# Message passing of a graph network: the block's own product opens its PSUM sum, a product of a zero column closes it

## The reference, cut to what matters

```python
h = node_embedding
for _ in range(DEPTH):                       # DEPTH = 3
    msgs = jnp.take(h, src, axis=0)
    msgs = jax.nn.relu(msgs @ W_edge + b_edge)
    agg = jax.ops.segment_sum(msgs, dst, num_segments=N_NODES)
    h = jax.nn.relu(jnp.concatenate([agg, h], axis=-1) @ W_agg + b_agg)
```

## Time and profile before

| | us |
|---|---|
| median of 3 runs | 6392.83 |
| the profiled execution's own time | 6391.64 |
| its span in the profile | 6389.9 |
| message passing, from the first to the last product L793 | 854.9 to 3439.8 |
| TensorE busy over the span | 4607.5 (72%) |
| GpSimd busy over the span | 3504.7 (55%) |

### The profile page before, as it was taken

How to read it: one execution, slowest core, us unless ns; L and a number is a source line. 1 busy time by engine, 2 the same in 40 slices (tenths; PEclk the granted TensorE clock), 3 DMA queues, 4 the chain that set the end, 5 groups by cost and what they waited for, 6 DMA issues and landing times. The chain is left out here.

```text
span 6389.9 us, 107350 instructions
## 1 busy us (share of the span) xinstructions
PE 4607.5 (72%) x19910; PEld 2847.6 (45%) x19911; DVE 3779.0 (59%) x12447; ACT 1894.9 (30%) x4118; POOL 3504.7 (55%) x3741
## 2 busy tenths in 40 slices
PE   5666657777677777667666777667777776888887
PEld 3444435555455555444443333334444443333333
DVE  7666633333333333333335888768888886777777
ACT  0222213333333333111111000022222222666666
POOL 1555544444344443444443555566666664888887
PEclk8888868888788888777778999955555556999999
DMA  0433435555445444433334888733333332333333
GB/s 29 132 129 127 132 111 156 154 152 151 135 149 153 150 149 146 117 106 109 107 106 129 269 268 270 253 88 99 99 98 99 100 98 76 103 105 105 105 105 94
DMA packets 732203, 840.14 MB, mean 131 GB/s; under 512 B 150205, under 2 KB 575272, under 8 KB 732068
## 3 DMA queue, kind: packets, MB, share of 16 engines
q1 hardware_dynamic: 619172, 619.89, 30.2%
q0 software_dynamic: 112896, 218.94, 13.4%
HBM read 439.86 MB, written 398.61 MB: 131 GB/s over the span
## 5 line engine op out<-in xcount | busy, mean ns | idle before, releaser
L756 POOL DMA_INDIRECT mp_gathered<-msg_rows,other_idx x1176 | 1116.6, 949 | 1463.7 <-PE bank L775 997.4
L775 PE MATMUL bank<-mp_edge_hot,mp_gathered 128*128 128x256 bf16 x5292 | 948.9, 310 | 517.9 <-issue 477.8
L775 PEld LDWEIGHTS bank<-mp_edge_hot,mp_gathered 128*128 x5292 | 558.8, 106 | 827.2 <-issue 718.1
L834 ACT ACTIVATE mp_h_out<-bank,mp_b_agg 128x256 f32<-128x256 f32 x588 | 278.5, 474 | 1488.9 <-PE bank L793 834.5
L522 POOL DMA_INDIRECT by_window<-so_pay,so_pos_i x392 | 394.0, 1005 | 426.3 <-issue 285.0
L868 DVE TENSOR_SCALAR mp_edge_hot<-digits,mp_first_col,column 128x256 bf16<-128x256 bf16 x1764 | 506.0, 348 | 144.5 <-PE bank L793 79.7
L793 PE MATMUL bank<-mp_h_in,mp_w_agg_h 128*128 128x256 f32 x1176 | 478.7, 495 | 110.2 <-issue 103.6
L1196 POOL DMA_INDIRECT at_kv<-kv_rows,kv_idx x392 | 387.4, 988 | 258.1 <-DVE at_prod L1350 141.5
L891 DVE TENSOR_TENSOR mp_msg_out<-mp_rest,mp_msg_out 128x256 bf16<-128x256 f32 x392 | 166.4, 424 | 590.4 <-ACT mp_msg_out L847 321.0
L1198 POOL DMA_INDIRECT at_q<-q_rows,node_idx x392 | 414.0, 1056 | 122.9 <-issue 122.9
L1475 POOL DMA_INDIRECT ff_agg<-at_rows,last_idx x392 | 413.9, 1056 | 98.6 <-issue 88.7
(11 more groups left out here) (216 smaller groups left out, 9177.7 us busy)
## 6 DMA issues: line engine op xcount, KB each, us to landing
mp_h_in<-h_cols SPq DMA_DIRECT2D x588, 128.0 KB
h_cols<-mp_h_out SPq DMA_DIRECT2D x588, 128.0 KB
msg_rows<-mp_msg_out SPq DMA_DIRECT2D x392, 192.0 KB
kv_rows<-pn_proj SPq DMA_DIRECT2D x98, 512.0 KB
msg_rows<-so_msg_out SPq DMA_DIRECT2D x98, 384.0 KB
h_cols<-so_h_out SPq DMA_DIRECT2D x98, 256.0 KB
pn_h_in<-h_cols SPq DMA_DIRECT2D x98, 256.0 KB
x_rows<-pn_x_b SPq DMA_DIRECT2D x98, 256.0 KB
```

The source lines that it names most:

```text
L756: pool.indirect_dma_start(gathered[:, r * PARTS * D:(r + 1) * PARTS * D], None, core.msg_rows[layer % 2], bass.IndirectOffsetOnAxis(ap=cor ...
L775: product = nc.tensor.matmul(agg_bank[k], gathered[:, bass.ds(at + d * D, D)], hot, start=(first and d == 0), stop=True, skip_group_check= ...
```

## The change

In `sum_edges` the fp32 product of the block's own columns now comes first and opens the sum. The wait for its operand `h_ld` comes with it, behind the wait for `h_ok`. The one-hot products follow, none of them with `start=True`. What closes the sum is a new bf16 product of 128 zero columns with one zero column into the first column of the bank; it adds zero and carries the increment of `win_mm`.

```diff
                         first, final = edge_tiles(pe, n, r, waits=False)
                         reached(pe, h_ok, wins + n - 1)
+                        pe.wait_ge(h_ld[r], 16 * (turns_done + j + 1))
+                        nc.tensor.matmul(agg_bank[r % 2], w_agg_h[:, :], h_in[r][:, :], start=True, stop=True, skip_group_check=True)
                         pe.wait_ge(edge_hot_ok, wins + n + 1)
                         pe.wait_ge(tile_in, layer * NT + first + ALWAYS)
                         for c in range(ALWAYS):
-                            added = add_tile(r % 2, first + c, edge_hot[r % HOTS][:, c, :], first=c == 0)
+                            added = add_tile(r % 2, first + c, edge_hot[r % HOTS][:, c, :])
                         added.then_inc(tile_mm[layer], 1)
                         further(pe, n, first, final, more)
-                        pe.wait_ge(h_ld[r], 16 * (turns_done + j + 1))
-                        nc.tensor.matmul(agg_bank[r % 2], w_agg_h[:, :], h_in[r][:, :], start=False, stop=True,
+                        nc.tensor.matmul(agg_bank[r % 2][:, 0:1], zero_cols[:, 0:D], zero_cols[:, 0:1], start=False, stop=True,
                                          skip_group_check=True).then_inc(win_mm, 1)
```

## The result

The changed kernel takes 6405.79 us in the median of 16 runs, the kernel before 6391.48 us in the median of 16 runs: the ratio is 1.0025, with a 95% interval from 1.0018 to 1.0031. That is +16 us by the ratio. The direction of the prediction was right and the time lies in its range; its size of +53 us was more than three times too large.

The account below looks back on a forecast made before the run. TensorE's sequencer, by its instruction count plus a slow stretch per chunk, was taken to bound message passing. Terms 41 + 15 - 3 = +53 us on 6391.64 us gave 6445 us (+0.8%), 80% range 6388 to 6500 us.

Parts of the forecast that it names:

- The bound: Message passing, some 2585 us: paced by the instructions TensorE's sequencer must issue, plus a slow stretch for each chunk.
- the order pays: Rival: the array ends the turn, so the product moved into idle gaps saves up to 139 us; 6311 us, chance 0.09.
- The lone waits: Blocks two to four of each turn: a semaphore wait becomes its own instruction, 0.10 us each, three a turn, +41 us.
- The closing product: End of each of 588 blocks: an added weight load and product at 0.025 us a pair, +15 us.
- The hold on `h_ok`: L786 at the block's head: no longer holding the sequencer on this semaphore gains 0 us; its records last 32 to 36 ns.
- the load's due time: Block's head: operand due 1.75 us earlier, 7.0 us after its load's issue; 0 us unless a load takes longer.
- Layer starts: The product runs while the first tiles come in, three times up to 1 us: -3 us, layer ends included.
- The step that failed: Turns beside gathers: the stretch set by the chunk's gathers keeps its length, so added instructions cost their fast price once.
- slow stretch: Part of each chunk beside gathers where TensorE's register instructions need from 1212.5 to 1217.3 us, some 0.69 us each.
- by number of instructions: Rival: the slow stretch counts instructions, not microseconds; 0.60 us a turn, 83 us, 6475 us (6500 with upper prices), chance 0.10.
- in slack: Rival: the turn's length hangs on the chunk, so added instructions cost only single microseconds; 6390 to 6395 us, chance 0.11.
- its last sign of being wrong: Loop turns: those with gathers grow by another amount than those without, so the slow stretch is no constant.

## Why the prediction had the direction right and the size wrong

**The bound** was read rightly (the mean of GpSimd's 133 waits is 7.5 us and not 7.4, which changes nothing). The sequencer's list is the turn: without gathers the change costs 54.9 us in time and 53.2 us between branches, and the array, which got 588 products more and a better order, takes no part in it there. The rival "the order pays" is out as a forecast, 6311 us against 6405.79 us. It priced one of a turn's four products, and what it names is there on a small scale: beside gathers on the first chip the new order gave back 13.5 us in two layers, where the prediction had the array get nothing back. Whether it is the idle array that pays was not isolated.

**The lone waits** were counted rightly (414) and priced somewhat low. On the first chip 368 of them cost 38 us, 0.10 us each, the value taken. Without gathers on the second the whole change comes to 0.129 us for each, and the start-to-start step is 0.125 to 0.126 us. The 0.1 us read for L50 in the earlier trace rows is a difference of two rounded times; unrounded it is 0.126 us (2557.695 to 2557.821). The rows would have allowed the upper bound of 0.13 us.

**The closing product** was priced too high. Forecast +15 us; measured -4 us [-8, +1] and +1 us [-6, +9]. The 0.025 us per pair of load and product was what remained of a stretch after an estimated step, and with steps of 0.115 us nothing remains. That the sum of 56 us was met without gathers is luck: one price was some 11 us too low and the other 15 us too high. The Trainium skill, "TensorE: Matmul & The Clock Gate", section "Wait — 56ns, not 53.3ns?", gives some 62 ns for each matmul with hardware decode off; the estimate of 36 us worked out from it lies further from the measured -4 and +1 us still.

**The hold on `h_ok`, at nothing,** was right: 0.9991 and 1.0006 without it. So was the load's due time. SyncE issued the load of the last block at 3445.10 us, its product started at 3452.35 us, and the sequencer went on at its pace.

**Layer starts, -3 us:** not to be seen. From the last branch of a layer to the first of the next it is 83.0 and 76.5 us before and 82.9 and 79.1 us after.

**The step that failed** is the one at the end of the sum: "I let it keep its length, so that the added instructions cost their fast price once." Beside gathers the five turns of the earlier trace rows grew by 0.16 us each in the place of 0.40, and all 132 by 0.09 us in the mean. So the turn is not the fast turn plus a slow stretch of constant length: the rest of it became shorter as instructions came in. Neither alternative that was named fits: by number of instructions the turn would have grown by 0.60 us, and the added work is not in slack, since lone waits still cost 19 to 31 us beside gathers. The prediction had named this itself as its last sign of being wrong, that the turn with gathers grows by another amount than the one without.

It is tempting to say that an added instruction is cheap in the slow stretch, where some register instructions last as little as 2 to 9 ns and not 36 to 46 ns. The trace of the changed kernel doesn't bear that out as the cause. Of its 414 lone waits in the loops, counted record by record, 319 last 51 ns, with a median step of 0.126 us to the sequencer's next own instruction; 66 last under 40 ns, 28 over 250 ns and one lies between. Two more traces of the same kernel give 310 and 327 in the place of 319. So three quarters of the waits pay the full price, 40 us by themselves, and yet the loops grew by 14.3 us. What was given back lies elsewhere in the turn.

Shown in its place is the amount: 55 us without gathers, 16 to 20 us with them; 13.5 us given back by the new order beside gathers where there is no slow stretch; and in the old order 19 us beside slow stretches for waits that come to 46 us at 0.126 us each. By what way the turn becomes shorter is open.

A block beside gathers in the changed kernel, PE's timeline from 1211 us, shows that the stretch itself looks as in the earlier trace rows: single one-hot products with "issue" ahead of each.

```profile
1214.71 0.28 PE L775 MATMUL bank<-mp_edge_hot,mp_gathered 128*128 128x256 bf16 x1 [0.96 <-issue]
1215.28 0.28 PE L775 MATMUL bank<-mp_edge_hot,mp_gathered 128*128 128x256 bf16 x1 [0.29 <-issue]
1216.00 0.39 PE L775 MATMUL bank<-mp_edge_hot,mp_gathered 128*128 128x256 bf16 x1 [0.43 <-issue]
1218.10 0.37 PE L775 MATMUL bank<-mp_edge_hot,mp_gathered 128*128 128x256 bf16 x1 [1.71 <-issue]
```

**Open** stays what the slow stretch is, why one of four chips has none, and why a turn beside gathers gives back part of what is added to it. The new order without any lone wait, in all three layers, was not run; with lone waits in the last layer alone it is even with the kernel before on three chips. No edit tried here beat the kernel before clear of noise.

## What to carry to other kernels

- Where a turn is paced by a sequencer, count its instructions, the waits first: two semaphores at one product make an instruction of 0.126 us at the sequencer's even pace, while a further small product behind others was free here. Put two waits on two neighbouring instructions that exist anyway.
- A price from a stretch in which the engine runs evenly can be right for each instruction and the sum still wrong. Here 6 of 138 turns ran without gathers; in the others most added waits paid the same price, and the turns grew by a quarter of it, because the rest of the turn did not keep its length.
- To separate the prices from what surrounds them, run both kernels once without the disturbing work (here the gathers), on the same chip: 54.9 us there against 20 us told at once that the sum of the prices was right and the account of the turns beside gathers was not.

## What the runs showed of the hardware that was not expected

The same kernel took 5306, 6388, 6508 and 6385 us on four chips. The first shows no slow stretch at all: register instructions at 36 and 46 ns and a granted clock of 1.00 beside the same gathers. In the run with the closing product alone, the loops of message passing go from 699 us (first branch) to 2385 us there, in place of 909 to 3429 us in the earlier trace rows, 834 us less; another 210 us less lie ahead of them. A difference of 17% between chips is some 70 times this change. Comparisons across chips would have told nothing, and even within a chip what the lone waits cost went from 38 us [31, 45] on the first to 31 [20, 44] and 24 us [15, 33] on the third and the fourth.
